# A recurrent block and a routed expert block: token groups of 1, 2, 2, 2 and 1 chunks, routing in pieces, expert weights split over ACT and POOL

## The reference

```python
Bu = einsum('bld,nd->bln', x, Bn);  states = lru_scan(lam, Bu)
y = einsum('bln,mn->blm', states, C).real + einsum('bld,md->blm', x, D_mat)
x = layernorm(x + x + sigmoid(res_logit) * (gelu(y @ W1) @ W2))
probs = softmax(x @ Wg);  weights, indices = top_k(probs, 2)
for e in range(8):
    h = gelu_exact(x @ W1[e] + b1[e])
    out = out + (h @ W2[e] + b2[e]) * cw[:, e:e+1]   # cw is 0 outside the top 2
return layernorm(x + out)
```

## Time and profile before

| | |
|---|---|
| Median of 3 runs | 338.85 us (338.72 to 339.04) |
| The profiled execution's own time | 338.63 us |
| Its span, first to last instruction | 336.6 us |
| Mean granted TensorE clock | 0.94 |
| Busy share of the span: PE, DVE, ACT, POOL | 81%, 69%, 63%, 65% |
| Chunks 1 to 7 begin on PE | 37.8 to 111.1 us |
| First and last tile transposed on PE | 122.6 and 284.7 us |
| POOL's sends of results | 186.8 to 305.1 us |

### The profile page before, as it was taken

The page is one execution under the profiler, slowest core; times in us unless marked ns, Lnnn a source line. Parts: engine busy times, 40 slices in busy tenths (PEclk is TensorE's granted clock), DMA queues, the critical chain, the costliest instruction groups (busy, mean ns, idle before and its releaser), DMA issues.

```text
span 336.6 us, 5255 instructions
## 1 busy us (share of the span) xinstructions
PE 271.1 (81%) x1287; PEld 210.6 (63%) x1287; DVE 231.3 (69%) x729; ACT 210.6 (63%) x458; POOL 220.2 (65%) x265
## 2 busy tenths in 40 slices
PE   2487999899998749737779699999999999981920
PEld 1333656556645527536679599999999999830400
DVE  3854739968869746916878678888888888600870
ACT  3512245644843745817769599999999999810380
POOL 3999196167778776700277777777777777772580
PEclk9997999999999959969979999999999999997875
DMA  4992010001111153324446465565556555315952
GB/s 89 331 333 74 1 33 1 0 16 49 48 47 39 50 153 115 118 57 179 167 125 242 160 208 198 176 222 195 183 196 219 198 178 177 118 47 177 375 157 62
DMA packets 31366, 46.39 MB, mean 138 GB/s; under 512 B 5097, under 2 KB 23025, under 8 KB 31337
## 3 DMA queue, kind: packets, MB, share of 16 engines
q1 hardware_dynamic: 25620, 35.97, 32.6%
q0 software_dynamic: 4832, 9.97, 8.9%
q10 hardware_dynamic: 884, 0.12, 0.2%
HBM read 16.99 MB, written 13.86 MB: 92 GB/s over the span
## 4 chain that ended last, share of the span: by engine, by line
POOL 45%; issue 18%; PE 13%; DVE 12%; DMA 6%; ACT 3%; SPq 0%; DVEq 0%; ACTq 0%; POOLq 0%
POOL results_d L460 27%; POOL slots_d L454 15%; PE bank L1076 3%; DVE work L694 3%; DVE early L973 1%; DMA late<-slots_d 1%; DMA slots_d<-rows,slot_i 1%; PE bank L1164 1%; PE bank L1053 1%; POOL rstd L443 1%; PE bank L1054 1%; DMA rows<-results_d 1%; DMA logs<-in_L_attn_nu_log_dram 1%; PE bank L1022 1%; PE bank L1055 1%
## 5 line engine op out<-in xcount | busy, mean ns | idle before, releaser
L460 POOL DMA_INDIRECT results_d<-work,dest x87 | 92.1, 1059 | 26.5 <-issue 26.5
L454 POOL DMA_INDIRECT slots_d<-rows,slot_i x64 | 65.6, 1025 | 41.5 <-DVE rows L833 21.9
L591 ACT ACTIVATE h<-bank,buse 128x384 f32<-128x384 f32 x116 | 68.0, 586 | 13.5 <-PE bank L1024 8.2
L924 DVE TENSOR_TENSOR h_l<-h,h_h 128x384 fp32r<-128x384 f32 x116 | 65.2, 562 | 15.7 <-ACT h_h L596 13.1
L1022 PE MATMUL bank<-h_h,wuse 128*128 128x384 f32 x116 | 45.0, 388 | 5.6 <-DVE h_l L924 5.4
L1022 PE MATMUL bank<-xbt_h,wuse 128*128 128x384 f32 x116 | 40.9, 353 | 2.3 <-ACT h L591 2.3
L1023 PE MATMUL bank<-xbt_l,wuse 128*128 128x384 f32 x116 | 39.7, 342 | 0.0
L1024 PE MATMUL bank<-xbt_h,wuse 128*128 128x384 f32 x116 | 39.6, 342 | 0.0
L1024 PE MATMUL bank<-h_h,wuse 128*128 128x384 f32 x116 | 39.6, 341 | 0.0
L1023 PE MATMUL bank<-h_l,wuse 128*128 128x384 f32 x116 | 39.4, 340 | 0.0
L528 ACT ACTIVATE h<-bank 128x512 f32<-128x512 f32 x32 | 18.8, 597 | 28.7 <-PE bank L1024 28.1
(11 more groups left out here) (199 smaller groups left out, 573.1 us busy)
## 6 DMA issues: line engine op xcount, KB each, us to landing
wuse<-fw SPq DMA_DIRECT2D x29, 512.0 KB, 3.4
late<-slots_d SPq DMA_DIRECT2D x29, 195.0 KB, 2.5
fw<-in_L_ffn_W_dram SPq DMA_DIRECT2D x16, 256.0 KB, 6.3
work<-in_L_attn_x3d_dram SPq DMA_DIRECT2D x8, 256.0 KB, 5.4
rows<-results_d SPq DMA_DIRECT2D x4, 512.0 KB, 5.3
work<-results_d SPq DMA_DIRECT2D x4, 512.0 KB, 8.6
out_dram<-fw SPq DMA_DIRECT2D x8, 256.0 KB, 2.3
slots_d<-zeros SPq DMA_DIRECT2D x9, 195.0 KB, 6.5
```

Of the source, the lines that this page charges most:

```text
L454: pool.indirect_dma_start(out=slots_d, out_offset=bass.IndirectOffsetOnAxis(ap=slot_i[:, k, i:i + 1], axis=0), in_=rows[:, k, i, :], in_of ...
L460: pool.indirect_dma_start(out=results_d, out_offset=bass.IndirectOffsetOnAxis(ap=dest[:, SQ * g + q:SQ * g + q + 1], axis=0), in_=yo[:, g ...
L591: act.activation(h32[:, b % 2, 0:SLOTS], H_PS[b % 2][:, 0:SLOTS], ACT.Gelu, bias=buse[:, k, b:b + 1]).then_inc(sm["gelu_b"], 1)
L924: dve.tensor_tensor(ht_l[b], h32[:, b % 2, 0:SLOTS], ht_h[b].bitcast(F32), ALU.subtract).then_inc(sm["hbl_ready"], 1)
```

## The change

The groups are chunks 0; 1 and 2; 3 and 4; 5 and 6; 7. Group g is routed in the chunk behind its last (chunks 1, 3, 5, 7), the last between the first tiles. With these sizes tile 0 is known with groups 0 and 1, tiles 1 to 5 with group 2, 6 to 10 with group 3, 11 to 28 with group 4. The tables of tiles are made in chunks 4 and 6, right behind the statistics, and before steps 2 and 6; the pieces of the last routing stand before steps 1, 3, 4 (the exponentials on ACT) and 5. The casts of the expert weights move to ACT, four in each of chunks 0 to 3, and the subtractions stay on POOL, where the dispatch of group 0 stands between the tenth and the eleventh. Later dispatches go in pieces of 4, 8 and 4 DMAs with a norm behind the first and the second. The product of mean and reciprocal deviation moves from POOL to DVE (`offsets`, behind `y_low`), where it waits for POOL's power; the operation for the negated mean is gone. PE transposes tile 0 behind chunk 7's products, not before its W2 products, and tile 1 within step 0. Slots are zeroed at tiles 6 to 9, not 4 to 7. Operations of the routing take the group's number of tokens, in the same order.

```diff
-GC = 2
+BOUNDS = (0, 1, 3, 5, 7, 8)
 FB = 4
 YO = 20
-TAILS = 4
...
-    NG = NCH // GC
-    GT = GC * QT
-    pairs = [2 * GT * P * (g + 1) for g in range(NG)]
+    NG = len(BOUNDS) - 1
+    GT = QT * max(b - a for a, b in zip(BOUNDS, BOUNDS[1:]))
+    pairs = [2 * QT * P * b for b in BOUNDS[1:]]
...
-            return (c - 2) // GC if c >= 2 and c % GC == 0 else None
+            return BOUNDS.index(c) - 1 if c in BOUNDS[1:] else None
+
+        def tokens_of(g):
+
+            return QT * BOUNDS[g], QT * (BOUNDS[g + 1] - BOUNDS[g])

...
-            sp.wait_ge(dispatched[0], 16 * 2 * GT)
+            sp.wait_ge(dispatched[0], 16 * 2 * tokens_of(0)[1])
             for n in range(PHASES):
                 if n:
+                    if n == 1:
+                        sp.wait_ge(sm["fw_lo"], NFW)
                     second_weights(begins[n] - 1)
                 if n == PHASES - 1:
                     sp.wait_ge(sm["prefilled"], 16)
                     sp.wait_ge(sm["tails_zero"], 16 * E)
                 sp.wait_ge(sm["route_ready"], n + 1)
-                sp.wait_ge(dispatched[n + 1], 16 * 2 * GT)
+                sp.wait_ge(dispatched[n + 1], 16 * 2 * tokens_of(n + 1)[1])
                 for g in range(begins[n], ends[n]):
                     load(g, g % 2)
-                    if g == 1:
-                        sp.wait_ge(sm["fw_lo"], NFW)
-                        second_weights(0)
                     if g == 2:
                         sp.wait_ge(sm["pre_a"], HB * NCH)
-                    if g >= 2 and g not in begins:
+                    if g not in begins:
                         second_weights(g - 1)
                     if TAILS <= g < TAILS + E // 2:
...
-            def weights(e, a):
-
+            for n in sizes:
+                last = pool.memset(restart[n][:, :].rearrange("p (e t) -> p e t", e=E)[:, :, 0:1], 0.0)
+            last.then_inc(sm["const_ready"], 1)
+
+            def weights_low(n):
+
+                e, a = divmod(n, 2)
+                pool.wait_ge(sm["fw_hi"], n + 1)
+                pool.tensor_tensor(fw_part(e, a, 1), fw_part(e, a, 1).bitcast(F32), fw_part(e, a, 0).bitcast(F32), ALU.subtract).then_inc(sm["fw_lo"], 1)
+
+            def norm(c):
+
+                pool.wait_ge(sm["ve_ready"], c + 1)
+                pool.tensor_tensor(rstd[:, QT * c:QT * (c + 1)], var_e[:], mhalves[:], ALU.pow).then_inc(sm["rstd_ready"], 1)
+
+            def dispatch(g, a, b):
+
+                t0 = tokens_of(g)[0]
                 if a == 0:
-                    pool.wait_ge(fw_loaded[e], 32)
-                n = 2 * e + a
-                raw = fw_part(e, a, 1).bitcast(F32)
-                pool.tensor_copy(fw_part(e, a, 0), raw).then_inc(sm["fw_hi"], 1)
-                pool.wait_ge(sm["fw_hi"], n + 1)
-                pool.tensor_tensor(fw_part(e, a, 1), raw, fw_part(e, a, 0).bitcast(F32), ALU.subtract).then_inc(sm["fw_lo"], 1)
-
-            def norm(c):
-
-                pool.wait_ge(sm["nm_ready"], c + 1)
-                wait(pool, sm["row0_ready"], c)
-                pool.tensor_tensor(rstd[:, QT * c:QT * (c + 1)], var_e[:], mhalves[:], ALU.pow).then_inc(sm["rstd_ready"], 1)
-                pool.wait_ge(sm["rstd_ready"], c + 1)
-                pool.tensor_tensor(nmr[:], nmean[:], rstd[:, QT * c:QT * (c + 1)], ALU.mult).then_inc(sm["nmr_ready"], 1)
-
-            def dispatch(g, half):
-
-                if half == 0:
                     pool.wait_ge(sm["routed"], g + 1)
-                    pool.wait_ge(sm["row1_ready"], GC * (g + 1))
-                for i in range(GT * g + QT * half, GT * g + QT * (half + 1)):
+                    pool.wait_ge(sm["row1_ready"], BOUNDS[g + 1])
+                for i in range(t0 + a, t0 + b):
                     for k in range(2):
...
-            for e in range(E):
-                for a in range(2):
-                    weights(e, a)
-                if e in (4, 6, 7):
-                    norm((4, 6, 7).index(e))
-            for g in range(NG - 1):
-                dispatch(g, 0)
-                if GC * g + 3 < NCH:
-                    norm(GC * g + 3)
-                dispatch(g, 1)
-                if GC * g + 4 < NCH:
-                    norm(GC * g + 4)
-            for half in range(GC):
-                dispatch(NG - 1, half)
+            for n in range(NFW):
+                if n in (4, 8, 12):
+                    norm(n // 4 - 1)
+                if n == 10:
+                    dispatch(0, 0, 4)
+                weights_low(n)
+            for g in (1, 2):
+                dispatch(g, 0, 2)
+                norm(2 * g + 1)
+                dispatch(g, 2, 6)
+                norm(2 * g + 2)
+                dispatch(g, 6, 8)
+            dispatch(3, 0, 2)
+            norm(7)
+            dispatch(3, 2, 8)
+            dispatch(4, 0, 4)
...
+            def weights_high(n):
+
+                e, a = divmod(n, 2)
+                act.wait_ge(fw_loaded[e], 32)
+                act.copy(fw_part(e, a, 0), fw_part(e, a, 1).bitcast(F32)).then_inc(sm["fw_hi"], 1)
+
...
+                if 4 * c < NFW:
+                    weights_high(4 * c)
+                    weights_high(4 * c + 1)
                 if c + 1 < NCH:
                     y_high(c + 1)
+                if 4 * c < NFW:
+                    weights_high(4 * c + 2)
+                    weights_high(4 * c + 3)
                 if c >= 1:
                     rows_of(c - 1)
                 if routed_in(c) is not None:
@@ -538,7 +552,7 @@

...
-            walk(act, MT, step, {1: lambda: rows_of(NCH - 1), 3: second_exp,
+            walk(act, MT, step, {2: lambda: rows_of(NCH - 1), 4: second_exp,
...
-                wait(dve, sm["nmr_ready"], c)
                 dve.tensor_scalar(var_e[:], mv[:, :, 1], EPS / 4, None, ALU.add).then_inc(sm["ve_ready"], 1)
-                dve.tensor_scalar(nmean[:], mv[:, :, 0], -1.0, None, ALU.mult).then_inc(sm["nm_ready"], 1)
+
+            def offsets(c):
+                dve.wait_ge(sm["rstd_ready"], c + 1)
+                wait(dve, sm["row0_ready"], c)
+                dve.scalar_tensor_tensor(out=nmr[:], in0=mv[:, :, 0], scalar=-1.0, in1=rstd[:, QT * c:QT * (c + 1)],
+                                         op0=ALU.mult, op1=ALU.mult).then_inc(sm["nmr_ready"], 1)

...
             def chunk(c):
-                g = routed_in(c)
+                g, ended = routed_in(c), routed_in(c - 1)
                 if c + 1 < NCH:
                     turn_back(c + 1, 0)
                     turn_back(c + 1, 1)
+                if ended is not None:
+                    route_weights(ended)
                 if c >= 1:
-                    if g is None and c >= 3:
-                        route_weights(routed_in(c - 1))
                     stats(c - 1)
                     aggregate(c - 1)
+                    if ended:
+                        route_tiles(ended - 1)
                     logits(c - 1)
                 if g is not None:
                     route_choice(g, 0)
@@ -738,70 +758,72 @@
                     route_hits(g)
                 if c + 1 < NCH:
                     y_low(c + 1)
+                if c >= 1:
+                    offsets(c - 1)
                 if g is not None:
                     route_exponents(g)
-                elif c >= 5:
-                    route_tiles((c - 5) // GC)
                 if c + 2 < NCH:
                     turn_in(c + 2)
                 if c == NCH - 1:
-                    first_tile()
+                    first_weights()
                 residual(c)
                 if g is not None:
                     route_ranks(g)
                     route_slots(g)

-            def first_tile():
+            def first_weights():
                 dve.wait_ge(sm["fw_lo"], NFW)
-                dve.wait_ge(sm["route_ready"], 1)
+                dve.wait_ge(sm["route_ready"], 2)
                 held.extend(expert_of(g) for g in range(2))
                 weights1(0, 0, held[0])
                 weights2(0, 0, held[0])
                 dve.wait_ge(sm["pre_a"], HB * NCH)
                 weights1(1, 1, held[1])
-                x_low(0, 0)
-                meta(0, 0)

...
+                t0, n = tokens_of(g)
...
+                dve.tensor_tensor(rows[:, 1, t0:t0 + n, D + 1], xex[:, n * E:n * (E + 1)], rden[:, 0:n], ALU.mult).then_inc(sm["routed"], 1)
...
+            x_low(0, 0)
+            meta(0, 0)
+            route_weights(NG - 2)
             stats(NCH - 1)
             aggregate(NCH - 1)
             logits(NCH - 1)
...
                 route_hits(NG - 1)
+                offsets(NCH - 1)
+
+            def next_tiles():
+                route_tiles(PHASES - 2)
+                dve.wait_ge(sm["route_ready"], PHASES - 1)

...
-            def last_weights():
-                route_weights(NG - 1)
+            def last_tiles():
                 route_tiles(PHASES - 1)
                 dve.wait_ge(sm["route_ready"], PHASES)

```

(34 more changed lines are left out.)

72 lines of the change are left out of this document (33 added, 39 removed).

## The result

The changed kernel took 340.02 us (median of 20 runs, 339.07 to 342.88), the kernel before beside it 338.65 (20 runs, 337.08 to 341.44): ratio 1.0053, interval 1.0033 to 1.0073. It is slower by half a per cent, and the forecast of 329.3, its range and its sign are wrong.

The account below looks back on a forecast made before the run. POOL's queue of dispatches and sends was taken to bound the kernel, PE next. Its last send, at 294.5 instead of 304.13, gave -9.6: 338.63 - 9.6 = 329.0, or 329.3 us with the runs' median 0.2 higher; range 323 to 337.

Parts of the forecast that it names:

- Part 2: Chunks 1 to 7: following POOL's queue of DMAs, subtractions and powers, about 4 of the start's 5.2 us are left.
- Part 1: Casts off POOL and the start: chunk 1 begins 5.2 us earlier, at 32.6; bounds 0 and 6.
- The start: Chunk 0 without POOL's weight work: faster DVE pair, less PE waiting and faster matmuls, 5.2 us in all.
- Rival A: The start gives nothing, since weight loads slow DVE or PE stays cold: 334 us, chance 0.18.
- D: No change: spread routing pieces between tiles stall PE, last weights come 10 us later: 338.7 us, chance 0.04.
- The powers: DVE waits in `offsets` for POOL's power, queued behind dispatches: 3.5 us late in chunk 3 and in chunk 7.
- The table and the pieces between the tiles: Last routing spread over six steps, added table 4.0 us: tile 2 at 134.3, tile 6 at 165.4.
- The end: POOL's queue: eight dispatches take 10.6 us, sends begin at 177.2, the last at 294.5 against 304.13.
- the sends' gain: POOL's last send begins at 294.5 instead of 304.13, behind 8 dispatches instead of 16: -9.6 us.
- C: Slower: DVE waits in `offsets` for powers behind slow dispatches, in chunks 4 to 7: 344 us, chance 0.08.
- B: Powers delay less than forecast, so PE's tiles begin 3 to 4 us earlier: 325 us, chance 0.16.

Follow-up runs that it names:

- e2: Changed kernel with POOL's 16 weight subtractions left out, a one-column fill in each one's place (low parts wrong): 326.42 us.
- e5: Changed kernel, whole computation, with the 16 weight subtractions made by DVE in places where it was seen idle: 328.09 us.
- e9: Kernel before, its groups, norms and table places kept, with weight casts on ACT and subtractions on DVE: 335.25 us.
- e4: Kernel before, its groups and routing kept, with weight casts on ACT and subtractions alone on POOL: 343.38 us.
- e8: Changed kernel with each POOL subtraction cut into four linked quarters of 128x128: 337.10 us.
- e10: As e8, but POOL makes the first group's dispatches and the third power before pieces 8 to 15: 338.43 us.
- e12: Changed kernel with each POOL subtraction waiting until all four casts of its chunk are done: 346.66 us.
- e11: As e5, but the first three tiles' results are sent back before the last group's dispatches: 325.23 us.
- e3: Changed kernel with weight casts and subtractions both on POOL as before, none on ACT, first dispatch behind all: 336.47 us.

## Why the prediction was wrong

**The step that failed** is in Part 2, in the price of the subtractions: "1.27 per subtraction (a median, 2.09 at most, with DVE in the way)". That is their price for POOL's list, and it was right (median 1.27 after). What they cost DVE I had read from the earlier trace rows, 1.52 us for two operations, and used only as a gain in chunk 0. Part 1 says that POOL has no weight work earlier, and never asks what stands beside it where it now is: the two choices of chunks 1 and 3, whose operations mostly have two SBUF operands and are chained one behind the other, with PE's ranks, the slots and the low part of y behind them. The trace of the kernel before has this very case, in chunk 2, where POOL's last subtractions (56.60 and 58.51) meet a choice:

```profile
55.70 0.22 DVE L783 TENSOR_TENSOR late<-early,s 128x64 f32<-128x64 f32 x1
...
58.80 1.06 DVE L783 TENSOR_TENSOR late<-early,s 128x64 f32<-128x64 f32 x1
```

With the price of the earlier trace rows, up to 0.76 us for an operation beside one subtraction, the ten of chunks 1 and 3 would have been some 8 us at once; measured were 13.6 in all (e2), 11.9 against the same work on DVE (e5). In the forecast's own terms, chunk 3 was to begin at 56.8 and chunk 7 at 108.6; they began at 63.77 and 118.45, and at 57.47 and 107.56 in e5. The page of the Trainium skill that I cited, SBUF — State Buffer, section SBUF: two separate sides, has the rule: a lock, held for the whole instruction, between a GpSimd operation and a DVE operation that is in a two-port mode, or that reads two SBUF operands while GpSimd's reads SBUF. The traces agree on which operations the subtractions hit: never `y_low`, nor the choice's reductions with their one operand (0.18 us at 39.82), but the scan and the choice's operations with two. They differ on the power, which reads SBUF too: two such operations beside it took their usual 0.19 us (38.03 and 38.25). And they differ on the length: 5.35 us is four instructions. I took from the rule only the half that ACT's casts cost nothing.

**The start** was right: chunk 1 on PE at 33.35 (I said 32 to 34; 32.04 in e2), and DVE's pair in chunk 0 took 1.29 for 2.80. Rival A falls. The first send came after 182, which I had as a sign of A or D; it was neither.

**The powers** had 3.5 us in chunk 3 and 3.5 in chunk 7. After, the first is hidden behind the long operations, so no run tests it as it was forecast: e2 and e5 have no subtractions in front of that power either. The second is 2.40 after, and nothing in e5, whose longest waits are 0.63 and 1.27, in chunks 4 and 5. The residual of chunk 7 was to begin at 124.0; it began at 120.6 in e5 and at 132.8 after.

**The table and the pieces between the tiles** were right: tile 2 to tile 6 was to take 31.1 us and takes 30.9 after (144.55 to 175.41) and 29.7 in e5.

**The end** was right in its lengths and wrong in its place. Eight dispatches were 10.6, and are 10.9; from first to last send I had 117.3, and it is 117.7; all of it begins 10.3 us late (187.5 for 177.2). That the sends' gain and the start were on record as one sum hid that both hang on chunks 1 and 3.

**The balance** in medians: weights off POOL -3.2 (e9), groups, pieces and tables -7.2 (e5 against e9), together -10.3 (e5 against before, rounded) where I had -9.6, though by the ratios the first is nearer to -4.5 and the second to -6; the subtractions on POOL and not on DVE +11.9. That is +1.6 by these, +1.4 measured. The casts on ACT cost at most some tenths of a us in a chunk: with them in place, e2's residuals of chunks 0 to 5 stand 11.7 to 12.5 us apart.

**The rivals.** C had the sign, and the wrong mechanism: dispatches have a median of 0.962 us after, 0.959 before. Its other half, the power behind dispatches, is real in e4, e8, e10 and e12. B, 325, is near what the kernel takes without its subtractions on POOL, but by another mechanism than B's. D had the last weights ten us late, as they were, but laid it on the pieces between the tiles, which took what they were forecast to. The chance for slower, 0.08, stood on one mechanism; a second one, in a row that I had read, was not priced at all.

## What to carry over

When work of POOL on SBUF is moved, list which DVE operations with two SBUF operands will run beside it, and who waits for them: a small operation in a chain pays for a whole subtraction of POOL, and in some places for several in a row. A contention that a trace shows where work is taken away must be charged where it is put. And a queue that bounds the end may have idle time earlier, into which some of its work can go (e11).

## What the runs showed of the hardware

- A DVE operation of 128x4 to 128x64 values with two SBUF operands, 0.15 to 0.26 us alone, took 1.0 to 1.3 us beside one POOL subtraction of 128x512 (1.27), and 3.25, 4.89 and 5.35 beside runs of two and four. A wait between the subtractions brought the longest down to 2.04. POOL lost nothing in these (1.25 to 1.28 for each subtraction in the changed kernel), but where DVE's scan was let through between two, the next subtraction took up to 2.20 (e4, e12).
- A copy from SBUF to SBUF (line 813) was hit too, 1.14 us for 0.17; reductions with one SBUF operand were not (0.18 at 39.82), nor operations with one operand in PSUM (0.68 inside a subtraction). POOL's casts hold DVE in the same way, for their own 0.6 us: 0.47 to 0.54 for operations of 0.17 to 0.22 (e3). The power did not: operations with two SBUF operands took their usual 0.19 and 0.22 beside it.
- A subtraction of a quarter of the columns took POOL 0.457 us, not a quarter of 1.27: four are 1.83, and with waits between them 2.1 to 2.6 (4.26 us for 8, 10.34 for 16).
